# The X projection of three scan units: four shifted matmuls against one plain projection with the convolution on VectorE

## What is computed

```
xz = x @ in_proj.T; xh, z = split(xz)            # 256 channels each
xc = conv_b + sum_k shift(xh, k) * conv_w[:, k]  # 4 taps, causal
xc = silu(xc)
dt, Bm, Cm = split(xc @ x_proj.T);  delta = softplus(dt @ dt_w.T + dt_b)
h[t] = h[t-1] * exp(delta[t] * A) + (delta[t] * xc[t]) * Bm[t]     # 16 states a channel
y = sum_s h * Cm + xc * D;  y = y * silu(z);  out = y @ out_proj.T
```

## Time and profile before

| | us |
|---|---|
| median of 3 runs | 626.09 (625.22 to 626.88) |
| profiled execution, its own time | 626.24 |
| span of its trace | 624.5 |
| unit 0, 1, 2, 3 in the trace (first scan to first scan) | 113.0, 114.0, 121.5, 113.2 |
| before the first scan; behind the last | 52.1; 110.7 |

### The profile page before, as it was taken

The page is one execution under the profiler, slowest core; times in us unless marked ns, Lnnn a source line. Parts: engine busy times, 40 slices in busy tenths (PEclk is TensorE's granted clock), DMA queues, the critical chain, the costliest instruction groups (busy, mean ns, idle before and its releaser), DMA issues.

```text
span 624.5 us, 9118 instructions
## 1 busy us (share of the span) xinstructions
PE 501.6 (80%) x3376; PEld 410.9 (66%) x3376; DVE 484.9 (78%) x635; ACT 448.3 (72%) x852; POOL 338.1 (54%) x156
## 2 busy tenths in 40 slices
PE   3386989978899998689989969698755578987697
PEld 3144856858688677677855758697644465877396
DVE  3765889858787786598799958989999996759632
ACT  2359867999978799899867899889778711570060
POOL 3013657868866676796766959677566681200000
PEclk9787999997899999799999999899999989787699
DMA  7030020222311122031321212222621121000101
GB/s 244 1 105 35 35 101 35 102 68 72 102 68 68 69 72 97 34 107 69 96 70 38 94 43 76 97 69 73 194 105 69 67 80 56 1 2 1 34 1 35
DMA packets 17884, 43.45 MB, mean 70 GB/s; under 512 B 1328, under 2 KB 7600, under 8 KB 17584
## 3 DMA queue, kind: packets, MB, share of 16 engines
q1 hardware_dynamic: 17840, 42.87, 20.2%
HBM read 41.56 MB, written 1.31 MB: 69 GB/s over the span
## 4 chain that ended last, share of the span: by engine, by line
PE 40%; ACT 26%; DVE 25%; issue 7%; POOL 1%; DMA 1%; DVEq 0%; ACTq 0%; POOLq 0%
ACT dBuT L552 12%; PE pro L1078 11%; PE yT L1082 8%; PE dBu L1082 8%; PE yT L1078 7%; DVE area L907 6%; ACT dA L545 6%; PE dBu L1078 4%; DVE area L903 4%; DVE area L936 3%; DVE top L934 3%; PE pro L1082 1%; DVE area L739 1%; ACT th L513 1%; ACT pre L520 1%
## 5 line engine op out<-in xcount | busy, mean ns | idle before, releaser
L462 POOL TENSOR_TENSOR hc<-area 128x1024 f32<-128x1024 f32 x128 | 309.4, 2420 | 153.7 <-DVE area L903 80.6
L552 ACT ACTIVATE dBuT<-area,bT 128x256 f32<-128x256 f32 x512 | 217.1, 499 | 42.4 <-PE dBu L1082 42.1
L1082 PE MATMUL dBu<-ident,dBuT 128*128 128x128 f32 x1024 | 148.1, 284 | 54.4 <-DVE area L907 31.4
L1082 PEld LDWEIGHTS dBu<-ident,dBuT 128*128 128x128 f32 x1024 | 118.7, 145 | 68.9 <-DVE area L907 37.7
L545 ACT ACTIVATE dA<-area,Aneg 128x1024 f32<-128x1024 f32 x128 | 146.1, 1143 | 3.6 <-DVE area L907 1.8
L1082 PE MATMUL yT<-ident,hc 128*128 128x128 f32 x1024 | 140.8, 283 | 0.0
L1082 PEld LDWEIGHTS yT<-ident,hc 128*128 128x128 f32 x1024 | 121.6, 146 | 18.1 <-issue 16.2
L907 DVE TENSOR_TENSOR_SCAN area<-dA,area,dBu 128x512 f32<-128x512 f32 x64 | 81.8, 1278 | 4.8
L903 DVE TENSOR_TENSOR_SCAN area<-dA,area,dBu 128x512 f32<-128x512 f32 x64 | 81.8, 1278 | 4.5 <-DVE area L903 0.5
L903 DVE TENSOR_TENSOR_SCAN area<-dA,dBu 128x512 f32<-128x512 f32 x64 | 77.1, 1205 | 10.3 <-PE dBu L1082 9.7
L907 DVE TENSOR_TENSOR_SCAN area<-dA,dBu 128x512 f32<-128x512 f32 x64 | 77.3, 1208 | 8.4 <-PE dBu L1082 7.6
(11 more groups left out here) (194 smaller groups left out, 594.6 us busy)
## 6 DMA issues: line engine op xcount, KB each, us to landing
area<-c_rows SPq DMA_DIRECT2D x64, 512.0 KB, 3.6
dBuT<-w_in SPq DMA_DIRECT2D x1, 2048.0 KB, 9.3
wp<-wpack_in SPq DMA_DIRECT2D x1, 1030.0 KB, 7.6
x<-x_in SPq DMA_DIRECT2D x2, 512.0 KB, 7.0
hc<-bcast_in SPq DMA_DIRECT2D x1, 1024.0 KB, 10.0
out<-x SPq DMA_DIRECT2D x4, 256.0 KB, 2.4
hT<-w_in SPq DMA_DIRECT2D x1, 512.0 KB, 8.3
acc<-w_in SPq DMA_DIRECT2D x1, 512.0 KB, 8.7
```

The costliest lines, as they stand in the source:

```text
L462: g_.tensor_tensor(hc[:, e % 3, :], hs[:, e % 3, :], Cb[:, g % 3, :], ALU.mult).then_inc(hc_done, 1)
L552: return nc.scalar.activation(dBuT[:, g % 2, n, :], duT[par][:, n, :], ACT.Copy, scale=bT[:, par, n, s:s + 1])
L1082: return nc.tensor.matmul(out, in_, ident[:, :] if idn is None else idn, start=start, stop=True, is_transpose=True, skip_group_check=True)
```

## The change

X items of the next unit become six pieces, three of 341 or 342 columns for each half. For a piece PE does one plain projection of the columns and the three before (or, backwards, behind) them, ACT's `item_a` scales it by the last tap and adds the bias into xc, DVE's `item_v` adds three taps one after another, each reading the PSUM bank and xc, with a wait between. One tile later on ACT `tanh_x` takes the tanh of the piece, and one more tile later DVE's `finish_x`, behind the second scan, multiplies. wtap, bias3, ones3, the bias parts and the transfer of the rows go. The items of a unit are laid out anew: two X pieces at tiles 0 and 1; then the four or six items of the other unit; X pieces 2 to 5; Z0 B0 Z1 B1 Z2 BT, DT0 to 3, Z3; DU always at tiles 25 to 28. Each item takes one tile.

```diff
-            items += [("X", 0, u + 1)]
+            items += [("X", 0, nxt), ("X", 1, nxt)]
             items += [(k, j, u - 1) for k, j in LAST_ITEMS] if u > 0 else [("Z", j, u) for j in range(4)]
-            items += [("X", j, u + 1) for j in range(1, 4)]
-            items += [("B", 0, u + 1), ("B", 1, u + 1), ("BT", 0, u + 1)]
-            items += [("DT", j, u + 1) for j in range(4)] + [("Z", j, u + 1) for j in range(4)]
-            items += [("DU", j, u + 1) for j in range(4)]
+            items += [("X", j, nxt) for j in range(2, NH * NX)]
+            items += [("Z", 0, nxt), ("B", 0, nxt), ("Z", 1, nxt), ("B", 1, nxt), ("Z", 2, nxt), ("BT", 0, nxt)]
+            items += [("DT", j, nxt) for j in range(4)] + [("Z", 3, nxt)]
...
+                if kind == "X":
+                    half, lo, hi = x_part(it)
+                    off = PAD if dr == 0 else 0
+                    at = dr * NH + half
+                    nc.scalar.activation(xc[par][:, half, lo:hi], src[:, off:off + hi - lo], ACT.Identity,
+                                         bias=biasc[:, at:at + 1], scale=convc[:, dr, half, DC - 1:DC]
+                                         ).then_inc(xacc_ready, 1)
...
+            def tanh_x(kind, j, u):
+
+                n = NH * NX * (u - 1) + j
+                half, lo, hi = x_part((kind, j, u))
+                wait_item(act, kind, j, u)
+                if n >= 2:
+                    act.wait_ge(x_ready, NH + n - 1)
+                nc.scalar.activation(thx[:, n % 2, 0:hi - lo], xc[unit(u)[2]][:, half, lo:hi],
+                                     ACT.Tanh).then_inc(thx_ready, 1)
...
+                if e >= 2 and ENDS[e - 2] is not None and ENDS[e - 2][0] == "X":
+                    tanh_x(*ENDS[e - 2])
                 if e and ENDS[e - 1] is not None:
                     item_a(*ENDS[e - 1])
...
+                    dve.wait_ge(xacc_ready, NH * NX * (u - 1) + j + 1)
+                    for k in range(DC - 2, -1, -1):
+                        off = k if dr == 0 else PAD - k
+                        ins = nc.vector.scalar_tensor_tensor(out, src[:, off:off + hi - lo], convc[:, dr, half, k:k + 1], out,
+                                                             ALU.mult, ALU.add)
+                        if k:
+                            step(ins)
+                        else:
+                            ins.then_inc(item_dve, 1)
...
+                dve.wait_ge(thx_ready, n + 1)
+                nc.vector.scalar_tensor_tensor(out, thx[:, n % 2, 0:hi - lo], 1.0, out,
+                                               ALU.add, ALU.mult).then_inc(x_ready, 1)
...
                 scan_chunk(e, 1)
+                if e >= 3 and ENDS[e - 3] is not None and ENDS[e - 3][0] == "X":
+                    finish_x(*ENDS[e - 3])
...
-                    at = c * CH + (part if dr == 0 else 2 * PAD - part)
-                    last = mm(dst, wtap[:, dr, part, half * P:(half + 1) * P], hT[:, b, at:at + CH], part == 0, False)
-                    if part == DC - 1:
-                        last = mm(dst, bias3[:, dr, half, :], ones3[:, 0:1].to_broadcast([3, CH]), False, True)
+                    if part == 1:
+                        half, lo, hi = x_part(it)
+                        at = lo if dr == 0 else lo + PAD
+                        last = mm(dst[:, 0:hi - lo + PAD], inx[:, dr, half * P:(half + 1) * P],
+                                  hT[:, b, at:at + hi - lo + PAD], True, True)
```

More of the change, by code:

```diff
@@ L34 @@
     WCOLS += _n
-CONVW_COLS = 2 * DC * DI
+NX = 3
+XLO = [L * c // NX for c in range(NX + 1)]
 FIRST_ITEMS = ([("B", 0), ("B", 1), ("BT", 0)]
@@ L54 @@
 assert len(CHOOSE_STEPS) == 2 * (TOPK // 8)
-def parts_of(kind):
-    return 4 if kind == "X" else 2
+DU_AT = 25
 def schedule():
@@ L85, in schedule @@
         parts[at + t] += [((k, j, NU - 2), 0), ((k, j, NU - 2), 1)]
-    ends = [[it for it, p in row if p == parts_of(it[0]) - 1] for row in parts]
+    ends = [[it for it, p in row if p == 1] for row in parts]
     return parts, [row[0] if row else None for row in ends]
@@ L161, in build_block @@
         du = yg
-        wtap = sb("wtap", [P, 2, DC, DI])
+        area4 = sb("area4", [P, 2 * DC * DI])
         Aneg = sb("Aneg", [P, 2, NH, DS])
@@ L414, in _ @@
             g_.memset(mhalf[:, :], -0.5).then_inc(s_c, 1)
-            g_.memset(ones3[:, :], 1.0).then_inc(s_c, 1)
             g_.memset(hT[:, :, :], 0.0).then_inc(s_c, 1)
@@ L439, in pool_du @@
                 wait_delta(g_, half, u)
-                for c in range(NCH):
-                    wait_item(g_, "X", half * NCH + c, u)
+                wait_x(g_, half, NCH - 1, u)
                 g_.tensor_tensor(du[:, half, :], delta[par][:, half, :], xc[par][:, half, :],
@@ L852, in item_v, with finish_x @@
                         nc.vector.tensor_tensor(dst, src, dst, ALU.add).then_inc(item_dve, 1)
+            def finish_x(kind, j, u):
+                n = NH * NX * (u - 1) + j
+                half, lo, hi = x_part((kind, j, u))
+                out = xc[unit(u)[2]][:, half, lo:hi]
+                dve.wait_ge(thx_ready, n + 1)
+                nc.vector.scalar_tensor_tensor(out, thx[:, n % 2, 0:hi - lo], 1.0, out,
+                                               ALU.add, ALU.mult).then_inc(x_ready, 1)
             def norm_stage(b, stage):
@@ L1109, in _ @@
             last.then_inc(gab_ready, 1)
-            def turn_parts():
-                pe.wait_ge(parts_ready, 1)
-                for k in range(NBIAS):
-                    last = turn(dBu[1][0:3, k * P:(k + 1) * P], part32[:, k, :], True)
-                last.then_inc(parts_turned, 1)
             def item_t(it, part):
@@ L1196, in item_t @@
                                       dr == 1 and h == 0, h == NH - 1)
-                if part == parts_of(kind) - 1:
+                if part == 1:
                     last.then_inc(pro_ready, 1)
@@ L1235, in _ @@
                     turn_xn(1)
-                for part in range(parts_of(k)):
+                for part in range(2):
                     item_t((k, j, 0), part)
             pe.wait_ge(ht_ready, 2)
-            turn_parts()
-            pe.wait_ge(bias_ready, 1)
-            pe.wait_ge(weights_ready, 1)
             pe.wait_ge(others_ready, 1)
```

92 lines of the change are left out of this document (36 added, 56 removed).

## The result

The change made the kernel slower: **653.82 us** (median of 4 runs, 649.63 to 655.09) against 626.49 (4 runs, 625.22 to 627.29) beside it on the same chip, a ratio of 1.0431 (95% interval 1.0403 to 1.0458). The forecast was 638.6 with a range of 628 to 648: the direction was right, the size was not. The profiled execution took 654.83, its span is 653.0.

A forecast was written before the change was run, and what follows sets the result against it. No engine was full; the limit changed by stretch: PE in unit 1's X stretch, DVE last or near it in the others', then ACT. Starts +2.0, X stretches +15.7, ACT stretches -5.2 made +12.5 on 626.24: 638.6 us, range 628 to 648.

The forecast's parts named there:

- Prices: Per operation in a piece: waited-for tap 0.61 us, product 0.51 (0.42 in the stream), Identity 0.64, tanh 0.45; DVE's total up about 31.
- An X tile of 4.6: A tile with a piece takes 4.6 us on DVE: two scans 2.5 plus the piece's 2.13.
- By a wide margin: DVE is last in all six piece tiles: 4.6 us against ACT 3.55, POOL 2.4 and PE 2.3.
- X stretches, +15.7: Tiles 7 or 8 to 16 of units 0, 1, 2 grow by 6.2, 2.0 and 7.5 us through DVE's load.
- My forecast has finish_x win: finish_x, issued right behind the second scan, starts 0.16 us before POOL's multiply and so is not held by it.
- Rival 2: POOL's multiply blocks finish_x; half of the 18 held at 1.9 us each, about +17, total 655 us; chance 0.12.
- The starts, +2.0: Tiles 0 to 7 of each unit, with pieces 0 and 1: +1.0, 0 and +1.0 us for units 0, 1, 2.
- the bank is free 1.1 later, behind three taps and not one product: At a unit's start y_start waits 1.1 us longer for the bank; PE's smaller load in tiles 0 and 1 offsets it.
- PE down by about 35: PE's busy time falls 11.5 us a unit, 35 in all, with a projection at 0.58 us.
- 0 to +2 for the clock: If PE ran at 1.2 GHz its work would just fill the new tiles, costing 0 to +2 us.
- ACT stretches, -5.2: From the X stretch to each unit's end: -1.5, -2.0, -1.7 us, from Z items moved out and less waiting behind softplus.
- Rival 1: PE's relief counts and DVE hides the taps, so the kernel gets faster, 618 us; chance 0.12.

The follow-up runs named there:

- experiment 7: The changed kernel with each plain projection done four times over into the same bank, result unchanged: 664.33 us.
- experiment 1: The changed kernel with finish_x ahead of the second scan in three tiles with side work (one in unit 0, two in unit 2): 653.37 us.
- experiment 2: The changed kernel with ACT's Identity of each unit's first piece issued at the front of its iteration, ahead of exp: 649.85 us, ratio 1.0363.
- experiment 6: The changed kernel with the three taps of a piece behind the second scan and finish_x, not between the scans: 656.07 us.
- experiment 3: The changed kernel with two of the three DVE taps of each piece left out, so the result is incomplete: 633.91 us, ratio 1.0112.
- experiment 10: The kernel before, in unit 0 alone with Z0 and Z1 between the B items and DU from tile 25: 626.37 us, ratio 0.9989.
- experiment 5: The changed kernel with both the early finish_x of experiment 1 and the early Identity of experiment 2: 644.94 us, ratio 1.0286.

## Why the prediction was wrong in size, step by step

- **Prices: right.** Tap, product, Identity and tanh came within 0.04 us, DVE's total at +31.0 for "about 31".
- **"An X tile of 4.6": slightly high.** 3.98 without a finish, 4.39 to 4.52 with one (tile 9 of unit 1, where DVE waits 1.03 for ACT's Identity, took 5.12). "By a wide margin" was wrong: PE, ACT and DVE hand one bank round in 3.4 us, which the forecast never added up; experiment 7 shows it as the next limit. In the steady tiles of the kernel after, at full clock, it is not the longest.
- **X stretches, +15.7 for +21.4.** By unit 6.2, 2.0, 7.5 for 8.5, 1.5, 11.5. The excess of 2.3 and 4.0 in units 0 and 2 goes with the held operations: one in unit 0 (3.37 for 1.20), two in unit 2 (4.4 together). With them gone the stretches lost 1.0 and 4.0 (experiment 1): all of the excess in unit 2, and about half in unit 0, where the rest stays open. The failed step is "My forecast has finish_x win": it did, in all 18 places, but the price was then looked for in the operation itself and not in the one behind it. The rows for this were at hand, since L884 held POOL in the kernel before; what POOL does to the operation after that was not asked. The Trainium skill, page "SBUF — State Buffer", section "Who interferes with whom", has the exclusion, and the trace agrees. Rival 2 named the lock, and that its total (655) is nearly the measured one is luck: it had "half of the 18" held for 17 us, none was, and 3 neighbours of theirs were, for 6.5; the rest of the miss lies at the starts.
- **The starts, +2.0 for +13.2: the largest miss.** The failed step is "the bank is free 1.1 later, behind three taps and not one product". It counted DVE's part of the hand-over and gave PE's lighter load against it. It left out that ACT reads the bank first and stands behind a whole iteration (experiment 2: 5.5 us by the starts, 4.0 by the medians), that PE's next dBu and y_add are queued behind the bank (experiment 6), and that PE, having idled, comes back at 1.2 GHz: granted clock 0.78, 0.90, 0.85 against 0.94, 0.95 and 1.00. Experiment 3 shows the starts falling by 12.7 when 6.8 us of taps go, and experiment 7 that 8.0 of the 13.2 stand in tile 1 whatever the clock.
- **"PE down by about 35": wrong, by 22.** A projection took 0.85 at full clock and 1.52 at 1.2 GHz, not 0.58 (0.58 is what each further one in the same group costs, experiment 7: (2.59 - 0.85) / 3), and much of PE's work ran longer at the lower clock (mean granted clock 0.94 before, 0.90 after; the transposes of dBu took 156.8 for 148.1, those of yT 144.9 for 140.8). The forecast's 0 to +2 for the clock stood on a stretch where the clock had stayed up; it did in unit 1's X stretch (1.00), and not in the others (0.89, 0.83) nor in the starts.
- **ACT stretches, -5.2 for -7.7:** right in sign, low by a third. Each item out of unit 0's stretch goes with 1.7 to 1.9 us, where the forecast had 0.45 for a Z item and a little for softplus (experiment 10); in unit 1 the count is not what decides.
- **Rival 1** fails as said: DVE's load shows, and even with 20.5 of the pieces' 38 us of DVE work gone (18 x 2.13) the kernel is 1.1% slower than before (experiment 3, 1.0061 to 1.0163).

Put together: 12.5 forecast, +6 in the X stretches (some 5 of it the held operations), +11 starts, -2.5 ACT stretches, +1.6 elsewhere are 28.6, the difference of the spans. Of the 11 at the starts 5.5 are ACT's late read (experiment 2). How the rest divides between PE's queue behind the bank and the clock is not shown; experiment 7 puts the clock's part of the starts' 13.2 at 5.2 or less.

## What to carry to other kernels

When work moves from one engine to three that pass one buffer round, add up the ring (0.85 + 0.62 + 1.79 here) and look where each reader stands in its own engine's order; the busy share of the relieved engine says nothing of it. Where tiles are filled and emptied (a unit's start), a dependent operation cost nearly twice its time here (12.7 for 6.8), so count it apart from the steady part. A new short operation with two SBUF inputs may lose nothing itself and let GpSimd in ahead of the next one, which then pays (3.37 for 1.20 here): look at what is issued behind it, or put a scan between the two, as experiment 1 does.

## What the runs showed that I had not expected

- An operation with one SBUF input can be held in the same way: in unit 0's tile 9 the first gate operation, L790, 128x256, took 2.45 us behind finish_x and POOL; the same one took 0.27 in the kernel before, where the next, L792, was the one held (2.50). The Trainium skill, page "SBUF — State Buffer", section "Who interferes with whom", names tensor_scalar among the operations that can take both ports; the trace agrees.

```profile
95.49 0.49 DVE L867 SCALAR_TENSOR_TENSOR area<-area 128x341 f32<-128x341 f32 x1
95.66 2.54 POOL L463 TENSOR_TENSOR hc<-area 128x1024 f32<-128x1024 f32 x1 [1.61 <-DVE area L919]
95.90 2.45 DVE L790 TENSOR_SCALAR acc<-acc 128x256 f32<-128x256 f32 x1
```

- Removing a wait can be invisible in the median of four runs of one kernel (experiment 1: 653.37 for 653.82, with 5.9 us less in three windows) and worth 4.9 us in another (experiment 5). The four runs of the changed kernel spread over 5.5 us, and those of the kernel before, which spread over 2.1 at first, over 6.5 in all experiments (624.94 to 631.4). The profiled executions differ most, outside what was edited, at the starts and behind the last scan, where the granted clock differs too; the fastest run of the changed kernel (649.63) has the highest mean clock, 0.918 for 0.901 to 0.908.
